# Layer 0 of a graph kernel: residual attention and the first convolution's tail written as one unrolled program over pairs of tiles

## The chip, the cores and the metric

The kernel runs on one core of a Trainium2 chip. The metric is the device time of one execution in microseconds, with the inputs already in HBM. The core has five engines that run their own instruction streams and meet at semaphores: TensorE (PE, with its weight loads PEld), VectorE (DVE), ScalarE (ACT), GpSimd (POOL) and SyncE (SP), which here only issues DMAs.

## The reference

3125 nodes with 256 features pass two layers. The change touches two blocks of layer 0, which both start from the same normalised rows `xn`:

```python
# residual attention ("mix"), linear attention with 8 heads of 32
t  = q @ kv / (q @ ksum + 1e-6)                    # q = elu(xn Wq) + 1
x1 = layer_norm(t + xn, ln1_g, ln1_b)
h  = gelu(x1 @ W1 + b1)
mix = layer_norm(h @ W2 + b2 + x1, ln2_g, ln2_b)

# two graph convolutions ("gnn"); the narrow width is 64
h  = (1 + eps_down) * (xn @ W1_down) + A @ (xn @ W1_down)
h  = relu(layer_norm(h, lng_down, lnb_down)) @ W2_down
x  = layer_norm(relu(h + xn + dir_emb[0]), ln1_g, ln1_b)   # the "down" tail ends here
h  = ... the same with A transposed, x @ W1_up, eps_up, W2_up ...
x  = layer_norm(relu(h + x + dir_emb[1]), ln2_g, ln2_b)    # the "up" tail

x_out = x_in + gnn + mix
```

The aggregation `A @ y` of the first convolution is computed while the adjacency tiles are built, before the two blocks here. After them comes the aggregation with the transposed adjacency, then the up tail, then experts, and a second layer of another make. Between the down tail and the next aggregation the new rows are multiplied by `W1_up` and the 64-wide result is split into three bf16 parts.

## The kernel before

The nodes are 25 tiles of 125 rows (`TILES`, `ROWS`), handled in 5 groups of 5 tiles (`GROUP`). The program is a row of stages. Each stage allocates its own memory and semaphores, opens with a barrier of all engines, and runs one instruction stream on each engine. The streams are loops on the chip: `overlapped` and `two_by_two` unroll two groups in a loop body, so that buffers alternate.

The stages around the change are, in order: `build_adjacency`, `mix_tail_l0` (tensors called mix_...), `gin_tail` with way "down" (gin_down_...), `gin_up` (up_...), and `gin_tail` with way "up" (gin_up_...). The mix stage starts with 8 loads of weights on SP and the down stage with 8 more. The engines of a stage wait for the last of its loads.

In `mix_tail_l0` VectorE divides the attention output by its denominators (L471 to L476), adds `XN` (L482), normalises, and later adds the MLP's output to the residual (L490), adds b2 (L493), normalises again and adds into `X` (L497). In `gin_tail` VectorE forms the hidden rows (L1050), normalises them, applies relu (L1054), and later adds the base rows (L1067), applies relu (L1071), normalises, moves the narrow product out of PSUM (L1079) and splits it (L124 to L130).

A normalisation is `layer_norm_stats` (L101, L104, L106: statistics, their aggregate, variance plus epsilon) and `layer_norm_affine`: for each tile one VectorE instruction subtracts the mean and multiplies by the gain (L113), ScalarE takes the square root of the group's variances (L507, L1094, L1103), VectorE takes the reciprocal (L115), and one more instruction for each tile multiplies by it and adds the shift (L118). GpSimd only copies slices of the queries (L451), adds the direction row (L1008) and copies rows out (L1013). The order on every engine is the order in which the code issues it; there is no scheduler.

## Time and profile before

| | us |
|---|---|
| median of 3 runs (2787.97 to 2790.32) | 2789.17 |
| the profiled execution, its own time | 2778.03 |
| its span, first to last instruction | 2776.3 |

Engine busy shares of the whole span: PE 76%, PEld 61%, DVE 58%, ACT 32%, POOL 12%. The mean granted TensorE clock is 0.848 of full speed. The profiled execution is 11 us shorter than the median of the runs, so differences are worked out inside the profile and then taken from the median. Stages follow one another at barriers, so the time of one stage adds to the total and the shares of the whole span say little about it; the stages are read one by one.

### The profile page before, as it was taken

What the parts mean: (1) busy time and instruction counts of PE and PEld (TensorE: products, weight loads), DVE (VectorE), ACT (ScalarE), POOL (GpSimd) and SP (SyncE); (2) the same over time, 40 slices, a digit from 0 to 9 for tenths busy, and PEclk for the clock granted to TensorE, in tenths of its full rate; (3) what the DMA queues carried; (4) which work ended last, traced back from release to release, by engine and by line L of the source; (5) the groups of instructions that cost most, each with busy time, mean ns of one, the idle gap of its engine ahead of it and who ended that gap; (6) DMA issues with size and microseconds to landing.
All of it is one profiled execution on the core that took longest, in us unless ns stands there. A gap on an engine that the chain in (4) does not pass through costs nothing. (4 is left out here: it accounts for less than half of the span.)

```text
span 2776.3 us, 43161 instructions
## 1 busy us (share of the span) xinstructions
PE 2098.0 (76%) x12626; PEld 1692.8 (61%) x12626; DVE 1600.5 (58%) x4311; ACT 902.2 (32%) x1696; POOL 336.9 (12%) x379
## 2 busy tenths in 40 slices
PE   7768887553577324899649779975999976899992
PEld 4446665342443214788526557754888865899992
DVE  4489997676720877322167622226999947344444
ACT  4335555121100011366425100004666631333330
POOL 0000000000100100344200000000000000333330
PEclk9889999676568555799869999988999985899996
DMA  2023333000045024122230033310222133422115
GB/s 59 10 79 113 125 122 124 17 0 9 0 124 160 6 69 118 44 66 65 59 87 0 6 104 90 90 53 25 56 57 66 34 98 130 159 93 70 48 43 150
DMA packets 90526, 196.52 MB, mean 71 GB/s; under 512 B 13526, under 2 KB 56267, under 8 KB 90452
## 3 DMA queue, kind: packets, MB, share of 16 engines
q1 hardware_dynamic: 75662, 161.01, 20.2%
q0 software_dynamic: 11520, 31.47, 3.6%
q10 hardware_dynamic: 3270, 3.20, 0.4%
q8 instruction: 28, 0.46, 0.1%
q14 instruction: 46, 0.38, 0.0%
HBM read 131.25 MB, written 64.39 MB: 70 GB/s over the span
## 5 line engine op out<-in xcount | busy, mean ns | idle before, releaser
L1572 PEld LDWEIGHTS experts_ps_h<-experts_xt,experts_up 128*128 128x128 f32 x2944 | 346.7, 194 | 28.2 <-issue 24.9
L1572 PE MATMUL experts_ps_h<-experts_xt,experts_up 128*128 128x128 f32 x2944 | 356.1, 278 | 4.4 <-ACT experts_xt L1606 2.5
L2221 PE MATMUL gat_ps_o<-Y,gat_prob_t 125*125 125x256 f32 x1250 | 273.9, 379 | 0.0
L1663 DVE COPY experts_up<-up 128x1024 f32 (+1 forms) x184 | 122.7, 696 | 243.6 <-ACT experts_hid L1616 167.1
L2221 PEld LDWEIGHTS gat_ps_o<-Y,gat_prob_t 125*125 125x125 f32 x1250 | 232.7, 188 | 33.7
L827 PE MATMUL adj_ps_w<-adj_one_k,adj_one_s 128*125 128x500 bf16 x1000 | 178.4, 305 | 80.2 <-DVE adj_one_k L758 57.8
L1584 PE MATMUL experts_ps_o<-experts_down,experts_hid 128*128 128x256 f32 x960 | 226.8, 380 | 0.3 <-ACT experts_hid L1616 0.3
L1901 PE MATMUL gcn_ps_a<-Yp,gcn_adj 125*125 125x512 bf16 x625 | 206.2, 383 | 20.9 <-DMA gcn_adj<-adjacency 11.0
L1584 PEld LDWEIGHTS experts_ps_o<-experts_down,experts_hid 128*128 128x128 f32 x960 | 173.2, 190 | 19.2 <-issue 0.5
L1631 ACT ACTIVATE experts_down<-down 128x1024 f32 (+1 forms) x120 | 138.8, 1157 | 138.9 <-DVE experts_out L1680 76.3
L827 PEld LDWEIGHTS adj_ps_w<-adj_one_k,adj_one_s 128*125 128x125 bf16 x1000 | 98.4, 138 | 130.3 <-DVE adj_one_k L758 58.0
L1902 PE MATMUL gcn_ps_b<-Yp,gcn_adj 125*125 125x256 bf16 x625 | 171.4, 274 | 0.0
L758 DVE TENSOR_SCALAR adj_one_k<-adj_key_row,adj_key_here 128x625 bf16<-128x625 f16 x500 | 159.7, 382 | 0.0
L1540 POOL DMA_INDIRECT pair<-experts_out,slot_dst x120 | 118.4, 986 | 326.4 <-DVE experts_out L1683 190.7
L1533 POOL DMA_INDIRECT experts_rows<-expert_rows,slot_src x120 | 117.2, 977 | 266.5 <-SPq L1486 127.9
L771 ACT ACTIVATE adj_tile<-adj_ps_w 125x500 bf16<-125x500 f32 x250 | 95.7, 437 | 153.9 <-PE adj_ps_w L827 153.9
L1606 ACT ACTIVATE experts_xt<-experts_ps_t 128x256 f32<-128x256 f32 x120 | 45.0, 375 | 264.9 <-PE experts_ps_t L1561 264.9
L1901 PEld LDWEIGHTS gcn_ps_a<-Yp,gcn_adj 125*125 125x125 bf16 x625 | 86.0, 138 | 73.3 <-issue 15.0
L1673 DVE TENSOR_TENSOR experts_hid<-experts_gate,experts_ps_h 128x512 f32<-128x512 f32 x64 | 44.0, 687 | 138.6 <-ACT experts_gate L1622 138.6
L2191 ACT ACTIVATE gat_prob_t<-gat_ps_t 125x500 f32<-125x500 f32 (+1 forms) x175 | 79.2, 566 | 120.1 <-PE gat_ps_t L2214 120.0
L1913 DVE TENSOR_TENSOR gcn_acc<-gcn_ps_a,Y 125x256 f32<-125x256 f32 x25 | 10.6, 424 | 166.8 <-PE gcn_ps_b L1902 166.8
L397 PE MATMUL front_ps_kv<-front_wkv,front_xt 128*125 128x512 f32 x200 | 98.1, 614 | 0.0
(363 smaller groups left out, 3811.4 us busy)
## 6 DMA issues: line engine op xcount, KB each, us to landing
adjacency<-adj_tile SPq DMA_DIRECT2D x25, 683.6 KB
adjacency_t<-adj_tile_t SPq DMA_DIRECT2D x25, 683.6 KB
up_adj_t<-adjacency_t SPq DMA_DIRECT2D x25, 683.6 KB
gcn_adj<-adjacency SPq DMA_DIRECT2D x25, 683.6 KB
cnt<-adjacency_t SPq DMA_DIRECT2D x25, 683.6 KB
up<-in_L_ffn_w SPq DMA_DIRECT2D x32, 512.0 KB, 4.7
combine_got<-pair SPq DMA_DIRECT2D x20, 560.0 KB
down<-in_L_ffn_w SPq DMA_DIRECT2D x16, 512.0 KB, 6.7
```

The lines of the kernel that those rows point to most:

```text
L397: last = nc.tensor.matmul(ps_kv[u % 2][0:ROWS, :], xt[b][:, k, cols], wkv[:, k, :], start=(k == 0), stop=(k == KC - 1))
L758: v.tensor_scalar(one_k[half][:, j, :], key_row[:], key_here[half][:, j:j + 1], None, ALU.is_equal).then_inc(one_ready, 1)
L827: last = nc.tensor.matmul(banks[bank][0:ROWS, 0:z - a], ones, keys[:, a:z], start=start, stop=stop)
L1533: nc.gpsimd.indirect_dma_start(out=rows[t % 8][:], out_offset=None, in_=table, in_offset=bass.IndirectOffsetOnAxis(ap=K.slot_src[:, t:t + ...
L1540: nc.gpsimd.indirect_dma_start(out=K.pair[:], out_offset=bass.IndirectOffsetOnAxis(ap=K.slot_dst[:, t:t + 1], axis=0), in_=out[t % 4][:], ...
L1572: last = nc.tensor.matmul(ps[:, h * 128:(h + 1) * 128], w[:, k * H + h * 128:k * H + (h + 1) * 128], xt[b][:, k, :], start=(k == 0), stop= ...
L1584: last = nc.tensor.matmul(ps_o[b][:, 0:C], hid[b][:, h * 128:(h + 1) * 128], downs[b][:, h * C:(h + 1) * C], start=(h == 0), stop=(h == HB ...
L1631: nc.scalar.activation(downs[r % 2][:], X.downs[:, bass.ds(place, 1), :].rearrange("p e w -> p (e w)"), ACT.Copy).then_inc(down_copied, 1)
L1663: last = nc.vector.tensor_copy(ups[r % 2][n][:], X.ups[n][:, bass.ds(place, 1), :].rearrange("p e w -> p (e w)"))
L1901: nc.tensor.matmul(ps_a[b][0:ROWS, :], w, K.Yp[:, s, 0:512], start=(s == 0), stop=(s == TILES - 1))
L1902: last = nc.tensor.matmul(ps_b[b][0:ROWS, 0:C], w, K.Yp[:, s, 512:768], start=(s == 0), stop=(s == TILES - 1))
L2221: last = nc.tensor.matmul(ps_o[b][0:ROWS, 0:C], prob_t[:, s * ROWS:(s + 1) * ROWS], K.Y[:, s, :], start=(s == 0), stop=(s == TILES - 1))
```

## The change

`mix_tail_l0` and the down half of `gin_tail` are gone. In their place `mix_and_down` runs both blocks in one stage, without loops on the chip. It works on pairs of tiles: 13 of them (`N`), the last a single tile. Every engine's stream is written as slots, `for s in range(-3, N + 6)`, and a slot holds the steps of different pairs (s + 3 to s - 5), so that a step's input was made some slots ago.

- The weights and vectors of both blocks (17 loads, class `MixDown`) are issued on SP at the start of `build_adjacency`, into memory of their own, and waited for at its end.
- VectorE takes the moments of each normalisation. GpSimd computes the inverse root, (variance + epsilon) to the power -0.5, in one instruction (L720 of the changed kernel). VectorE multiplies it by the negative mean. ScalarE then normalises, one activation for each tile with these two as scale and bias.
- Gain and shift of the mix normalisation, of the hidden one and of the down tail's are applied by ScalarE when it moves the transposed rows out of PSUM, where they are per-partition values. Where the rows are also needed untransposed, GpSimd multiplies by the gain (L728, L733, L744). The shifts are folded into rows added elsewhere: b2 and ln1_b enter the MLP's second matmul as a product with a row of ones, ln1_b of the convolution and ln2_b of the mix block are added to the up tail's vectors.
- GpSimd also adds into `X` (L738) and adds the direction row (L750). ScalarE moves the narrow product out of PSUM (L685, L686).
- `gin_up_tail` is the old tail's "up" half, with two more loads and two small additions at its start.

```diff
-            mix_tail_l0(nc, K, D)
-            gin_tail(nc, K, "gin_down", D, "down", K.XN, K.X1)
+            mix_and_down(nc, K, D)
             gin_up(nc, K)
-            gin_tail(nc, K, "gin_up", D, "up", K.X1, None)
+            gin_up_tail(nc, K, D)
...
+            def moments(s, n, src, which):
+                dve.drain()
+                for u in range(n):
+                    v.bn_stats(stats[:, u, :], src[:, u, :])
+                dve.drain()
+                for u in range(n):
+                    v.bn_aggr(mv[:, u, :], stats[:, u, :])
+                dve.drain()
+                v.tensor_scalar(neg[which][:, s % 4, 0:n], mv[:, 0:n, 0], -1.0, None, ALU.mult)
+                v.tensor_scalar(var[which][:, s % 4, 0:n], mv[:, 0:n, 1], LN_EPS, None,
+                                ALU.add).then_inc(var_ready[which], 1)
+
+            def shifts(s, which):
+                n = tiles(s)[1]
+                dve.wait_ge(rstd_ready[which], s + 1 + START)
+                v.tensor_tensor(shift[which][:, s % 4, 0:n], neg[which][:, s % 4, 0:n], rstd[which][:, s % 4, 0:n],
+                                ALU.mult).then_inc(shift_ready[which], 1)
...
+            for s in range(-3, N + 6):
+                if live(s + 3):
+                    hidden(s + 3)
+                if live(s - 3):
+                    shifts(s - 3, OUT)
+                if live(s - 2):
+                    moments(s - 2, tiles(s - 2)[1], res[(s - 2) % 3], OUT)
+                if live(s - 1):
+                    shifts(s - 1, ROW)
+                if live(s + 1):
+                    add_input(s + 1)
+                if live(s + 3):
+                    moments(s + 3, tiles(s + 3)[1], hid[(s + 3) % 3], HID)
+                if live(s + 1):
+                    moments(s + 1, tiles(s + 1)[1], att[(s + 1) % 3], MIXED)
+                if live(s + 2):
+                    shifts(s + 2, HID)
+                if live(s + 1):
+                    rows(s + 1)
+                if live(s - 5):
+                    split(s - 5)
+                if live(s):
+                    relu(s)
+                    moments(s, tiles(s)[1], row[s % 3], ROW)
+                if live(s + 1):
+                    shifts(s + 1, MIXED)
+                if live(s + 2):
+                    heads(s + 2)
+                if live(s - 1):
+                    residual(s - 1)
...
+            def normalise(s, dst, src, which, done):
+                act.wait_ge(shift_ready[which], s + 1 + START)
+                for u in range(tiles(s)[1]):
+                    last = nc.scalar.activation(dst[:, u, :], src[:, u, :], ACT.Identity,
+                                                bias=shift[which][:, s % 4, u:u + 1],
+                                                scale=rstd[which][:, s % 4, u:u + 1])
+                last.then_inc(done, 1)
...
+            for s in range(-3, N + 6):
+                if live(s - 4):
+                    rows_turned(s - 4)
+                if live(s + 1):
+                    hidden(s + 1)
+                if live(s - 1):
+                    mixed_turned(s - 1)
+                if live(s - 5):
+                    narrow(s - 5)
+                if live(s):
+                    mixed(s)
+                if live(s + 1):
+                    hidden_turned(s + 1)
+                if live(s - 3):
+                    out(s - 3)
+                if live(s - 1):
+                    gelu(s - 1)
+                if live(s - 1):
+                    rows(s - 1)
...
+            def root(s, which):
+                n = tiles(s)[1]
+                pool.wait_ge(var_ready[which], s + 1 + START)
+                p.tensor_tensor(rstd[which][:, s % 4, 0:n], var[which][:, s % 4, 0:n], half[:, 0:n],
+                                ALU.pow).then_inc(rstd_ready[which], 1)
...
+            for s in range(-3, N + 6):
+                if live(s - 1):
+                    root(s - 1, ROW)
+                if live(s - 4):
+                    add_out(s - 4)
+                if live(s):
+                    mixed_gain(s)
+                if live(s - 2):
+                    root(s - 2, OUT)
+                if live(s - 3):
+                    out_gain(s - 3)
+                if live(s + 3):
+                    root(s + 3, HID)
+                if live(s + 1):
+                    root(s + 1, MIXED)
+                if live(s - 1):
+                    row_gain(s - 1)
+                if live(s + 3):
+                    direction(s + 3)
...
+            for s in range(-3, N + 6):
+                if live(s - 1):
+                    up(s - 1)
+                if live(s):
+                    turn(s, ps_m, z1[s % 2], z1_done, x1t_done, m_done)
+                if live(s + 1):
+                    rows(s + 1)
+                if live(s - 3):
+                    turn(s - 3, ps_g, zr[(s - 3) % 3], zr_done, xt_done, g_done)
+                if live(s - 4):
+                    narrow(s - 4)
+                if live(s + 2):
+                    attention(s + 2)
+                if live(s - 1):
+                    out(s - 1)
+                if live(s + 2):
+                    hidden(s + 2)
```

The four loops over `s` are, in this order, those of VectorE, ScalarE, GpSimd and TensorE.

On VectorE, in `mix_tail_l0`, one group of 5 tiles is normalised like this in the kernel before (mix_x_1 is the normalised buffer):

```order
L482 TENSOR_TENSOR mix_att<-mix_att,XN 125x1280
L101 BN_STATS mix_stats<-mix_att 125x6 x5
L104 BN_AGGR mix_mv<-mix_stats 125x2 x5
L106 TENSOR_SCALAR mix_var_eps<-mix_mv 125x5
L113 SCALAR_TENSOR_TENSOR mix_x_1<-mix_att,mix_mv,mix_vec 125x256 x5
L114 REGISTER_ALU
L115 RECIPROCAL mix_rstd<-mix_std 125x5
L118 SCALAR_TENSOR_TENSOR mix_x_1<-mix_x_1,mix_rstd,mix_vec 125x256 x5
```

and a pair of the changed kernel, in the middle of a full slot, like this:

```order
L540 TENSOR_TENSOR md_att<-md_att,XN 125x512
L505 BN_STATS md_stats<-md_hid 125x6 x2
L508 BN_AGGR md_mv<-md_stats 125x2 x2
L510 TENSOR_SCALAR md_neg<-md_mv 125x2
L511 TENSOR_SCALAR md_var<-md_mv 125x2
L505 BN_STATS md_stats<-md_att 125x6 x2
L508 BN_AGGR md_mv<-md_stats 125x2 x2
L510 TENSOR_SCALAR md_neg<-md_mv 125x2
L511 TENSOR_SCALAR md_var<-md_mv 125x2
L517 TENSOR_TENSOR md_shift<-md_neg,md_rstd 125x2
L564 TENSOR_TENSOR md_row<-md_ps_w,md_base 125x512
```

The two passes over the rows (L113, L118) are gone from VectorE; a multiplication of two columns (L517) has come, and steps of other pairs stand between the moments and it.

On GpSimd the whole work of one group in the down stage is, in the kernel before (the ISA row is a wait):

```order
L1008 ISA
L1008 TENSOR_TENSOR gin_down_base_d<-XN,gin_down_direction 125x1280
L1012 REGISTER_ALU
L1013 REGISTER_ALU
L1013 COPY X<-gin_down_row 125x1280
```

and one slot of the changed kernel has this (in order: direction, root, add_out, mixed_gain, root, out_gain, two roots, row_gain; X stands for `X` in L738 and for `X1` in L744):

```order
L750 TENSOR_TENSOR md_base<-XN,md_wide 125x512
L720 TENSOR_TENSOR md_rstd<-md_var,md_half 125x2
L738 TENSOR_TENSOR X<-X,md_z_1 125x512
L728 TENSOR_TENSOR md_zg<-md_z_1,md_wide 125x512
L720 TENSOR_TENSOR md_rstd<-md_var,md_half 125x2
L733 TENSOR_TENSOR md_z_0<-md_z_0,md_wide 125x512
L720 TENSOR_TENSOR md_rstd<-md_var,md_half 125x2 x2
L744 TENSOR_TENSOR X<-md_zr,md_wide 125x512
```

GpSimd has gone from two instructions a group to five wide ones and four roots a pair, all in one queue, and the roots stand between the wide ones.

## Rows read from the trace of the kernel before

**Rows 1.** Busy time by engine in three stretches: mix stage, gap, down stage.

```profile
core 0: us, PE busy (x) PEld busy (x) DVE busy (x) ACT busy (x) POOL busy (x), PEclk, DMA share, GB/s
...
497.00:656.00 159.00, 87.19 (x330) 65.42 (x330) 118.09 (x360) 31.69 (x61) 3.68 (x3) 0.70 0.00 0
656.00:667.00 11.00, 0.00 (x0) 0.00 (x0) 0.00 (x0) 0.00 (x0) 0.00 (x0) 0.50 0.18 53
667.00:794.00 127.00, 62.53 (x225) 50.29 (x225) 91.08 (x277) 12.79 (x40) 21.49 (x10) 0.50 0.00 0
```

**Rows 2.** Timeline at the ends of the two stages (start, duration, instruction, idle before).

```profile
485.19 0.42 SPq L440 DMA_DIRECT2D mix_w<-in_L_mix_W  x1
...
497.11 2.12 PE L532 MATMUL mix_ps_a<-kv,QT 128*125 128x132 f32 x8 [19.38 <-DMA mix_vec<-in_L_mix_b]
...
793.01 0.49 DVE L130 TENSOR_TENSOR Yp<-gin_down_rest,Yp 125x320 bf16<-125x320 f32 x1
794.95 0.33 SPq L56 DMA_DIRECT2D up_adj_t<-adjacency_t  x1
```

**Rows 3.** Timeline of SP's transfers around the start of the adjacency stage.

```profile
128.76 0.42 SPq L622 DMA_DIRECT2D adj_dst_rows_i<-in_dst_rows  x1
166.66 0.36 SPq L56 DMA_DIRECT2D adjacency<-adj_tile  x1
```

**Rows 4.** Timeline of VectorE, one normalisation of the mix stage.

```profile
506.30 1.73 DVE L101 BATCH_NORM_STATS2 mix_stats<-mix_att 125x6 f32<-125x256 f32 x5
508.10 0.44 DVE L104 BATCH_NORM_AGGREGATE mix_mv<-mix_stats 125x2 f32<-125x6 f32 x5
508.62 0.17 DVE L106 TENSOR_SCALAR mix_var_eps<-mix_mv 125x5 f32<-125x5 f32 x1
508.70 2.06 DVE L113 SCALAR_TENSOR_TENSOR mix_x<-mix_att,mix_mv,mix_vec 125x256 f32<-125x256 f32 x5
```

**Rows 5.** Groups of instructions in the mix stage (busy us, mean ns).

```profile
L490 DVE TENSOR_TENSOR mix_att<-mix_ps_o,mix_x 125x256 f32<-125x256 f32 x25 | 10.6, 424 | 24.8 <-PE mix_ps_o L552 24.8
...
L507 ACT ACT_TABLE_LOAD x6 | 7.7, 1283 | 30.2 <-DVE mix_var_eps L106 30.1
L482 DVE TENSOR_TENSOR mix_att<-mix_att,XN 125x1280 f32<-125x1280 f32 x5 | 7.6, 1524 | 0.9 <-issue 0.8
```

**Rows 6.** Groups of instructions in the down stage.

```profile
L1008 POOL TENSOR_TENSOR gin_down_base_d<-XN,gin_down_direction 125x1280 f32<-125x1280 f32 x5 | 15.4, 3080 | 117.3 <-SPq L972 117.3
...
L1067 DVE TENSOR_TENSOR gin_down_row<-gin_down_ps_o,gin_down_base_d 125x512 f32<-125x512 f32 (+1 forms) x15 | 9.0, 602 | 13.8 <-PE gin_down_ps_o L1127 13.8
...
L1071 DVE TENSOR_SCALAR gin_down_row<-gin_down_row 125x1280 f32<-125x1280 f32 x5 | 4.1, 827 | 0.5
...
L126 DVE TENSOR_TENSOR gin_down_rest<-Y,Yp 125x320 f32 (+1 forms) x5 | 2.5, 492 | 0.4
```

**Rows 7.** Groups of GpSimd, whole span.

```profile
L674 POOL TENSOR_TENSOR adj_two_parts<-adj_parts 125x64 f32<-125x64 f32 x25 | 10.8, 432 | 300.4 <-ACT adj_parts L789 300.4
```

**Rows 8.** Timeline of VectorE and GpSimd together, down stage.

```profile
690.07 1.25 POOL L1013 COPY X<-gin_down_row 125x1280 f32 x1 [19.72 <-DVE gin_down_row L118]
690.14 1.52 DVE L1050 SCALAR_TENSOR_TENSOR gin_down_hid<-Y,gin_down_eps,AGG 125x320 f32 x1 [0.23 <-issue]
691.28 3.13 POOL L1008 TENSOR_TENSOR gin_down_base_d<-XN,gin_down_direction 125x1280 f32<-125x1280 f32 x1
...
693.07 1.38 DVE L106 TENSOR_SCALAR gin_down_var_eps<-gin_down_mv 125x5 f32<-125x5 f32 x1
```

**Rows 9.** Timeline of the up tail: the hidden rows with GpSimd idle.

```profile
917.19 0.55 DVE L1050 SCALAR_TENSOR_TENSOR gin_up_hid<-Y,gin_up_eps,AGG 125x320 f32 x1 [1.53 <-PE gin_up_ps_h L1119]
```

**Rows 10.** Timeline of TensorE: an MLP product at full clock, three products at half.

```profile
518.05 4.41 PE L157 MATMUL mix_ps_t<-mix_x1t,mix_w 128*128 128x500 f32 x16
...
677.12 4.62 PE L1127 MATMUL gin_down_ps_o<-gin_down_w,gin_down_hid_t 64*125 64x256 f32 x10 [0.91 <-ACT gin_down_hid_t L1097]
...
690.04 2.34 PE L139 MATMUL gin_down_ps_t<-ident_f,gin_down_row 125*128 125x125 f32 x10 [8.30 <-DVE gin_down_row L118]
...
693.87 4.46 PE L1140 MATMUL gin_down_ps_y<-gin_down_wy,gin_down_xt 128*125 128x64 f32 x20 [1.49 <-ACT gin_down_xt L148]
```

More of the change, by code:

```diff
@@ L503, in _ @@
[L503 to L518 removed]
+            p = nc.gpsimd
@@ new lines, in direction @@
+            def direction(s):
+                t, n = tiles(s)
+                if s >= 3:
+                    pool.wait_ge(row_done, s - 2 + START)
+                p.tensor_tensor(base[s % 3][:, 0:n, :], K.XN[:, t:t + n, :], wide(3, s), ALU.add).then_inc(base_done, 1)
+            for s in range(-3, N + 6):
[17 more added lines that the diff above has]
+                    direction(s + 3)
@@ new lines, in hidden @@
+            def hidden(s):
+                pe.wait_ge(zh_done, s + 1 + START)
+                if s >= 1:
+                    pe.wait_ge(hid_t_done, s + START)
+                if s >= 6:
+                    pe.wait_ge(y_done, s - 5 + START)
+                for u in range(tiles(s)[1]):
+                    last = nc.tensor.transpose(ps_s[0:64, u * ROWS:(u + 1) * ROWS], zh[s % 2][:, u, :],
+                                               K.ident_f[0:ROWS, 0:ROWS])
+                last.then_inc(hid_done, 1)
@@ L965, in _, with gin_up_tail @@
                                         AX.X, ALU.add)
-def gin_tail(nc, K, stage, D, way, base, out):
-    first = way == "down"
+def gin_up_tail(nc, K, D):
     with ExitStack() as st:
-        m = Memory(nc, st, stage)
+        m = Memory(nc, st, "gin_up")
         w2 = m.sb("w2", (64, C))
-        wy = m.sb("wy", (128, KC, 64))
         eps1 = m.sb("eps1", (ROWS, 1))
@@ L1042, in _ @@
             v.tensor_scalar(eps1[:], eps1[:], 1.0, None, ALU.add)
-            if first:
-                v.memset(K.Yp[:, :, 192:256], 0.0)
+            v.tensor_tensor(direction[:], direction[:], extra[:, 0, :], ALU.add).then_inc(joined, 1)
+            v.tensor_tensor(wide[:, 1, :], wide[:, 1, :], extra[:, 1, :], ALU.add)
             dve.drain()
```

470 lines of the change are left out of this document (290 added, 180 removed).

## The prediction, on record before the changed kernel ran

> **What bounds the kernel now.** I read the busy times by stretch first, since stages meet at barriers. The mix stage computes from 497 to 656 us and the down stage from 667 to 794, with 11 us of nothing but loads between them and 12 ahead of the first [rows 1, 2]. In both VectorE is the busiest engine: 118.1 of 159 us and 91.1 of 127, against TensorE's 87.2 and 62.5 [rows 1]. The views of waits and the timelines say what the rest is: VectorE waits 24.8 us for the MLP's last product and 13.8 us for the down stage's rows [rows 5, 6], because within a group of five tiles the steps follow one another and little of the next group is mixed in. The region that the change replaces, from the first load at 485.19 to the first transfer of the next stage at 794.95 [rows 2], lasts 309.8 us.
>
> **What VectorE does after the change.** A full slot handles one pair of tiles in each step. Its price, from rows, with 0.07 us for each gap behind a drain (506.30 + 1.73 to 508.10) [rows 4]:
>
> - Moments of 256 columns: five statistics take 1.73 us, so two about 0.74 (the first costs a bit more than the following ones); aggregates of two 0.23 (of five 0.44); negative mean and variance 0.25 together (one is 0.17); three gaps 0.22 [rows 4]. That is 1.44, three times 4.32. With 64 columns I take 1.04. Together 5.36.
> - Four multiplications of two columns, like L106's 0.17 with a little for their waits: 0.8 [rows 4].
> - Hidden rows of 128 columns: 320 columns take 0.55 with GpSimd idle [rows 9], so 0.34.
> - Adding the input, 512 columns: 1280 take 1.52, about 1.04 ns for a column and 0.18 fixed [rows 5]: 0.71, with its gap 0.78.
> - Residual and base rows out of PSUM, 512 columns each: 15 instructions took 9.0 us, ten of them with 512 columns and five with 256, so 0.69 and 0.42 [rows 6]: 1.38.
> - Relu of 512 columns: 1280 take 0.83 [rows 6], so 0.43 and 0.07: 0.50.
> - Splitting: three operations of 128 columns, L126 with 320 took 0.49 [rows 6], so 0.29 each and two gaps: 1.07.
> - Heads: an operation of 256 columns out of PSUM takes 0.42 (L490) [rows 5], two overlapped 0.8; denominators, reciprocal and gaps 0.5: 1.31.
>
> The sum is 11.54 us a pair. For 12.5 pairs that is 145 us where VectorE is busy 209.2 now [rows 1]. The difference is mainly L113 and L118, 2.06 us for five tiles each [rows 4], three times over the wide rows and once over the narrow. To 11.54 I add 0.5 for some 15 satisfied waits.
>
> **What GpSimd's new work costs VectorE.** A wide operation of GpSimd takes 3.08 us for 1280 columns and 0.43 for 64 [rows 6, 7], so 1.3 for 512; five make 6.5 us a slot. The power has no row. Its floor is the 0.2 us that the smallest operations take; upward I take 0.43, the small addition [rows 7], for the sum, and say below where it would hurt. So GpSimd needs 8.2 us of a slot and isn't the bound. But it blocks VectorE. At 690.14 the hidden rows took 1.52 us instead of 0.55 while a GpSimd copy ran to 691.32, and at 693.07 L106 took 1.38 instead of 0.17, until GpSimd's addition ended at 694.41 [rows 4, 8, 9]; the statistics between them were not slowed. So an operation of VectorE of either kind waits for the whole GpSimd instruction. Going through a slot in program order I find four such meetings. mixed_gain becomes free when residual ends and takes its turn just ahead of the first shifts: 1.25. out_gain ends during the hidden moments: 0.5. row_gain and direction stand back to back where the split wants to run: 0.8 and 1.2. add_out falls under heads, which read PSUM, and costs nothing. That is 3.75, less 0.2 each (the rows show a little less delay than overlap), so 3.0 us a slot. Bounds: 0, and 6.5 if all five block fully. I take 3.0 since each meeting follows from the order.
>
> The Trainium skill (SBUF — State Buffer, Who interferes with whom) says the same in general, that VectorE instructions with two SBUF inputs or in a two-port mode and GpSimd's exclude each other for a whole instruction; by it the additions of two SBUF tensors block as well, which no row here shows clearly, and the sum would keep its 3.0. Against the change stands its page GPSIMD Engine Reference, Engine selection: two-input elementwise work is about twice as slow on GpSimd and belongs on VectorE. The rows agree on the price, 3.08 us against 1.52 for 1280 columns [rows 5, 6]. What they make of it here: kept on VectorE, the five would cost 5 x 0.71 = 3.6 us a slot, against 3.0 of blocking, so moving them gains little; the gain comes from L113 and L118, which go to ScalarE.
>
> **A slot, and the stage.** 11.5 + 0.5 + 3.0 = 15.0 us. Twelve full pairs 180, the single last tile 8.4, the operations ahead of the loop 1.3. The first slots have enough steps of their own to keep VectorE busy. In the last ones only chains are left (transposes, move, narrow product, move, split): some 6 us idle. Stage: 196 us.
>
> **The cover.** ScalarE has 17 activations a slot, about 7 us, and its table of functions is changed once, where the square root's alone was loaded six times (1.28 us each [rows 5]). TensorE's products a slot have 3576 columns, 8 + 2 transposes and 4 narrow products. At half clock (each product is recorded twice) 1280 columns took 4.62 us, ten transposes 2.34, ten narrow products 4.46 [rows 10]: 12.9 + 2.3 + 1.8 = 17.0. At full clock 2500 columns took 4.41 [rows 10], so about 8.4. The granted clock was 0.70 in the mix stage with PE busy 55% and 0.50 in the down stage with 49% [rows 1], so I expect about 0.75 and some 11 us a slot, hidden. The chain through the engines is covered too: out(s - 1) can start some 3 us into VectorE's slot, when gelu is done, and is wanted at 14.3; even at half clock it takes 5.5. The roots of MIXED are wanted 4 us after their variance.
>
> **The ends.** Loads: they move to `build_adjacency`, where SP issues nothing between 129.2 and 166.7 us [rows 3], so they cost nothing there; 485.19 to 497.11, 11.9 us, goes [rows 2], less 1.6 for opening the stage with 23 more semaphores (an estimate: 0.07 us each, from the two stages before and after the down stage, which open 2.1 and 1.5 us after the last operation with 18 and 9 semaphores). The gap between the stages, 11 us [rows 1], goes entirely. 1.5 us from the last operation to the next stage stay [rows 2]. After: 1.6 + 196 + 1.5 = 199, so the region falls by 111. The up tail gets two more loads, two additions of 0.42 and a change of table: +2. Net -109. The profiled execution would be 2778 - 109 = 2669, the median **2680**.
>
> **Rivals.**
> - GpSimd doesn't get in the way: 0 instead of 3.0 a slot, 39 us less, 2641. For it: half of VectorE's slot reads PSUM or takes statistics. Against: rows 8.
> - TensorE sets the pace, at half clock throughout: 17.0 and one wait of 1.4, so about 18 a slot, +3 in twelve slots: 2717. For it: the down stage never got above 0.50 [rows 1]. Against: such a TensorE would never pause, and it was granted 0.70 and more when it was busy 55%.
> - The roots are late, a wait in place of the removed one: power, signal and queue on GpSimd put some 3 us on two of the four chains of a slot, 20 to 21 us a slot: about 2750. For it: a root stands behind wide operations.
> - Slower than before: the power is a long routine on GpSimd. VectorE's slot would have to reach 15.0 + 109/12.5 = 23.7 us; GpSimd reaches that when four powers take 23.7 - 6.5 = 17.2 us, 4.3 us each, ten times the small addition. With 6 us each a slot is 30.5, so 15.5 x 12.5 = 194 more than forecast: 2874. Against: it handles two columns.
> - The stage is as long as before, since work only moved: would need 24 us a slot with nothing in the rows to fill it.
>
> **How the numbers follow.** VectorE bound with blocking, slots of 13.5 to 17.5 us, 2660 to 2712: 0.65. No blocking, 2641: 0.10. TensorE at 2717: 0.10. Late roots, 2750: 0.09. Slower: 0.05. Unchanged: 0.01. The range takes the first three and the bounds of their terms: 2640 to 2728, and leaves out the last three. 0.2% (5.6 us) is about what a measurement of this kernel can tell from no change. Faster 0.94, within it 0.01, slower 0.05.
>
> **What the new profile would show.** A stage of about 196 us between the adjacency's end and the next aggregation; VectorE without long waits in it, some 165 to 190 us busy because blocked instructions read longer; the first shifts and the split at over 1 us where GpSimd's gain runs; bn_stats at 0.41 unchanged; powers near 0.4; TensorE's clock near 0.75; no load wait in front. The prediction is wrong if VectorE's waits for ScalarE or GpSimd (L517) come to more than 1 us a slot, if a power takes over 2 us, or if SP's added loads delay the adjacency's first steps.

## The result and the profile after

The changed kernel takes **2664.44 us** (median of 4 runs, 2661.84 to 2667.41) against 2789.45 for the kernel before on the same chip: a ratio of 0.9553 with a 95% interval of 0.9538 to 0.9567. The prediction was 2680 with a range of 2640 to 2728, so the sign and most of the mechanism were right, and the forecast time was 15.6 us too long.

The kernel before was profiled a second time (e9 below), and this execution, 2790.22 us, is nearer to the median than the first. The comparison below uses it. These are busy times by stretch, cut at the same places in both kernels: the replaced stages (from their first load, or the merged stage's first VectorE operation), the next aggregation, the up tail's loads, the up tail, and the rest. The columns are the stretch, its length, the busy time of each engine with its instructions, the granted TensorE clock, the DMA share and GB/s. First the kernel before, second execution:

```profile
486.10:795.67 309.57, 149.63 (x555) 115.83 (x555) 209.32 (x637) 44.47 (x101) 26.40 (x14) 0.60 0.02 6
795.67:903.61 107.94, 95.75 (x403) 44.97 (x403) 3.88 (x7) 3.15 (x7) 0.00 (x0) 0.85 0.70 181
903.61:913.63 10.02, 0.00 (x0) 0.00 (x0) 0.16 (x2) 0.00 (x0) 0.00 (x0) 0.50 0.16 51
913.63:1010.67 97.04, 30.85 (x75) 18.30 (x75) 83.88 (x255) 5.78 (x20) 15.23 (x5) 0.50 0.00 0
1010.67:2788.50 1777.83, 1451.65 (x8659) 1245.72 (x8659) 929.27 (x2185) 611.84 (x1041) 254.15 (x263) 0.88 0.26 73
```

The changed kernel:

```profile
488.26:662.97 174.71, 147.84 (x629) 106.81 (x629) 151.77 (x514) 93.49 (x218) 115.02 (x118) 0.79 0.00 1
664.54:772.26 107.72, 93.86 (x403) 44.74 (x403) 3.88 (x7) 3.15 (x7) 0.00 (x0) 0.86 0.70 182
772.26:785.02 12.76, 0.00 (x0) 0.00 (x0) 0.82 (x3) 1.28 (x1) 0.04 (x1) 0.50 0.18 60
785.02:881.52 96.50, 30.85 (x75) 18.37 (x75) 83.56 (x255) 5.79 (x20) 15.13 (x5) 0.50 0.00 0
881.52:2660.10 1778.58, 1452.08 (x8659) 1246.68 (x8659) 929.30 (x2185) 612.14 (x1041) 255.03 (x263) 0.88 0.25 73
```

The next aggregation starts at 664.54 instead of 795.67, 131.1 us earlier. The 309.6 us became 174.7, and 1.6 more to the next stage's first transfer; of what that saves, 2.0 are lost because the stage takes longer to open and 0.2 because the adjacency ends later. The aggregation itself is the same, 107.9 and 107.7. The up tail's loads take 12.8 instead of 10.0, its work half a microsecond less, and what follows to the end of the execution's own time 0.8 more (1780.3 against 1779.5). 131.1 + 0.2 + 0.5 - 2.7 - 0.8 = 128.3; the two executions differ by 2790.22 - 2661.84 = 128.4. VectorE's busy time in the stage fell from 209.3 to 151.8 us and TensorE's did not change (149.6 and 147.8). TensorE is now busy 85% of the stage instead of 48%, and its granted clock went from 0.60 to 0.79. VectorE is busy 87%.

Of the 134.9 us between 309.6 and 174.7, 57.5 are VectorE's busy time and 77.4 its idle time: the loads at the two places ([rows 1, 2]: 11 us and 12) and, for the larger part, waits for other engines within a group of tiles. No run here prices the pairs and slots apart from the rest; e5 below, with the normalisation back on VectorE, is still 94.8 us shorter than the old stages.

The loads cost the adjacency little, but not nothing. VectorE's first cast behind the adjacency's own three loads, first in e9 and then in the changed kernel:

```profile
132.55 0.38 DVE L685 CAST adj_src_f<-adj_src_i 128x420 f32<-128x420 int32 x1 [7.53 <-DMA adj_dst_rows_i<-in_dst_rows]
...
132.96 0.38 DVE L999 CAST adj_src_f<-adj_src_i 128x420 f32<-128x420 int32 x1 [8.31 <-DMA adj_dst_rows_i<-in_dst_rows]
```

The first of those loads is issued at 128.13 in e9 and at 127.84 in the changed kernel, so the cast comes 4.4 us behind it before and 5.1 us after: the 17 loads queued behind them delay the adjacency's first steps by 0.7 us. Its last operation on GpSimd starts at 480.30 in e9 and at 480.45 here, which is 0.4 us later counted from the first load. That operation, and VectorE's first of the merged stage:

```profile
480.45 0.19 POOL L992 COPY DEG<-adj_parts 125x1 f32<-125x1 f32 x1
...
488.26 0.15 DVE L498 TENSOR_SCALAR md_eps<-md_eps 125x1 f32<-125x1 f32 x1 [14.85 <-PEq L85]
```

One VectorE slot, from one residual addition to the next (start, duration):

```profile
584.82 0.68 DVE L548 TENSOR_TENSOR md_res<-md_ps_o,md_zg 125x512 f32<-125x512 f32 x1
585.42 0.34 DVE L555 SCALAR_TENSOR_TENSOR md_hid<-Y,md_eps,AGG 125x128 f32<-125x128 f32 x1
585.68 1.24 DVE L517 TENSOR_TENSOR md_shift<-md_neg,md_rstd 125x2 f32<-125x2 f32 x1
587.02 0.75 DVE L505 BATCH_NORM_STATS2 md_stats<-md_res 125x6 f32<-125x256 f32 x2
...
588.56 0.69 DVE L540 TENSOR_TENSOR md_att<-md_att,XN 125x512 f32<-125x512 f32 x1
...
590.08 0.37 DVE L510 TENSOR_SCALAR md_neg<-md_mv 125x2 f32<-125x2 f32 x1
...
592.93 1.14 DVE L577 CAST Yp<-md_rest 125x128 bf16<-125x128 f32 x1
594.15 1.22 DVE L579 TENSOR_TENSOR Yp<-md_rest,Yp 125x128 bf16<-125x128 f32 x1
...
598.55 0.68 DVE L548 TENSOR_TENSOR md_res<-md_ps_o,md_zg 125x512 f32<-125x512 f32 x1
```

GpSimd in the same slot:

```profile
584.35 1.27 POOL L738 TENSOR_TENSOR X<-X,md_z 125x512 f32<-125x512 f32 x1
585.64 1.27 POOL L728 TENSOR_TENSOR md_zg<-md_z,md_wide 125x512 f32<-125x512 f32 x1
588.49 0.70 POOL L720 TENSOR_TENSOR md_rstd<-md_var,md_half 125x2 f32<-125x2 f32 x1 [1.57 <-DVE md_var L511]
589.15 1.27 POOL L733 TENSOR_TENSOR md_z<-md_z,md_wide 125x512 f32<-125x512 f32 x1
...
592.73 1.27 POOL L744 TENSOR_TENSOR X<-md_zr,md_wide 125x512 f32<-125x512 f32 x1
593.95 1.27 POOL L750 TENSOR_TENSOR md_base<-XN,md_wide 125x512 f32<-125x512 f32 x1
```

The slot lasts 13.73 us and VectorE has no wait in it. Four VectorE instructions are long: a shift of two columns takes 1.24 us beside `mixed_gain`, L510 0.37 at the end of `out_gain`, the two last operations of the split 1.14 and 1.22 beside `row_gain` and `direction`. [rows 8] showed the same in the kernel before, once with each kind of instruction. Beside a power (588.49) an addition of 512 columns took its usual 0.69. VectorE's only waits for another engine behind its first instruction of the stage all fall in the drain, the last slots in which few steps are left (engine, line, what for: us in total, times, longest):

```profile
DVE md_res L548 <- PE md_ps_o L814: 2.6, 3, 1.1
```

GpSimd's powers, from the groups of instructions of the stage (busy us, mean ns | idle before):

```profile
L720 POOL TENSOR_TENSOR md_rstd<-md_var,md_half 125x2 f32<-125x2 f32 (+1 forms) x52 | 35.9, 690 | 53.1 <-DVE md_var L511 53.1
```

### The profile page after: what moved, and what is told of

Same layout as the page of the kernel before. It is cut to its first block and busy times, and to the rows that moved or that the text cites. A ratio compares the mean times of both kernels' runs of the same rounds, so it can differ in the third digit from the quotient of the medians.

```text
span 2660.1 us, 43432 instructions
## 1 busy us (share of the span) xinstructions
PE 2101.0 (79%) x12700; PEld 1688.1 (63%) x12700; DVE 1544.3 (58%) x4190; ACT 952.5 (36%) x1814; POOL 426.6 (16%) x483
## 5 line engine op out<-in xcount | busy, mean ns | idle before, releaser
L1943 DVE TENSOR_TENSOR experts_hid<-experts_gate,experts_ps_h 128x512 f32<-128x512 f32 x64 | 44.0, 687 | 140.1 <-ACT experts_gate L1892 129.8
L2183 DVE TENSOR_TENSOR gcn_acc<-gcn_ps_a,Y 125x256 f32<-125x256 f32 x25 | 10.6, 424 | 166.0 <-PE gcn_ps_b L2172 166.0
```

## Experiments

All but e9 are edits of the changed kernel. The median is of four runs; the ratio is to runs of the kernel before on the same chip, which had medians of 2788.6 to 2791.7. "Stage" is from VectorE's first operation to its last (174.7 us in the changed kernel), in one profiled execution of each kernel. How well it repeats can be seen from e4, whose stage is the same program from its first VectorE operation on: 174.8. A full slot is one in which every step has a pair; it is read from one residual addition to the next. In this table clock and busy times are of the stage. e3 and e12 leave work out and do not compute the reference's result.

| | median us | ratio, 95% | stage us | full slot us | PE / DVE busy us | clock |
|---|---|---|---|---|---|---|
| changed kernel | 2664.4 | 0.9538 to 0.9567 | 174.7 | 13.7 to 14.0 | 147.8 / 151.8 | 0.79 |
| e1 shifts later | 2661.6 | 0.9524 to 0.9565 | 177.2 | 13.1 to 14.0 | 146.8 / 145.7 | 0.80 |
| e2 split first | 2665.0 | 0.9530 to 0.9573 | 177.4 | 11.6 to 14.3 | 146.6 / 140.1 | 0.81 |
| e3 short GpSimd | 2634.7 | 0.9426 to 0.9462 | 146.9 | 10.6 to 10.9 | 127.8 / 121.4 | 0.91 |
| e4 loads back | 2674.0 | 0.9567 to 0.9602 | 174.8 | 13.7 to 14.0 | 148.0 / 151.9 | 0.79 |
| e5 normalise on VectorE | 2701.2 | 0.9663 to 0.9712 | 214.8 | 16.9 to 17.3 | 154.1 / 190.5 | 0.75 |
| e6 roots twice | 2671.4 | 0.9567 to 0.9618 | 182.6 | 14.1 to 14.4 | 149.3 / 157.6 | 0.78 |
| e7 = e2, up twice | 2660.3 | 0.9527 to 0.9582 | 171.7 | 12.6 | 148.2 / 142.3 | 0.93 |
| e8 all on VectorE | 2667.7 | 0.9550 to 0.9597 | 183.4 | 13.8 to 14.1 | 149.8 / 157.9 | 0.79 |
| e10 up twice alone | 2662.7 | 0.9518 to 0.9566 | 174.1 | 13.7 to 14.1 | 150.8 / 152.6 | 0.90 |
| e11 direction on TensorE | 2686.5 | 0.9596 to 0.9654 | 193.7 | 11.9 to 15.3 | 175.5 / 135.4 | 0.75 |
| e12 no bias product | 2659.7 | 0.9518 to 0.9550 | 171.5 | 12.6 | 131.9 / 142.3 | 0.78 |

### e3: how much GpSimd's wide operations cost VectorE

```diff
-                p.tensor_tensor(zg[s % 2][:, 0:n, :], z1[s % 2][:, 0:n, :], wide(0, s), ALU.mult)
+                p.tensor_tensor(zg[s % 2][:, 0:n, 0:2], z1[s % 2][:, 0:n, 0:2], wide(0, s), ALU.mult)
 (the same in the other four; base, zg and X1 are filled with zeros at the stage's start)
```

> Leaves work out: GpSimd's five wide operations handle 2 columns of a tile instead of 256; the rest of their outputs is filled with zeros once at the stage's start (3 to 6 us, which the trace shows apart). Theory A (3.1 us a slot of blocking): VectorE's slot falls to about 10.6 us, the stage by 39 us before the filling, 2630. Rival (forecast: no blocking): 2664 plus the filling, 2668. Theory C (TensorE close behind): slots of 11.6 us with VectorE waiting for TensorE, 2640.

The same place in the slot, VectorE, with short GpSimd operations:

```profile
576.27 0.23 DVE L579 CAST Yp<-md_rest 125x128 bf16<-125x128 f32 x1
576.57 0.29 DVE L581 TENSOR_TENSOR Yp<-md_rest,Yp 125x128 bf16<-125x128 f32 x1
...
580.04 0.68 DVE L550 TENSOR_TENSOR md_res<-md_ps_o,md_zg 125x512 f32<-125x512 f32 x1
...
580.90 0.17 DVE L519 TENSOR_TENSOR md_shift<-md_neg,md_rstd 125x2 f32<-125x2 f32 x1
...
590.93 0.68 DVE L550 TENSOR_TENSOR md_res<-md_ps_o,md_zg 125x512 f32<-125x512 f32 x1
```

The shift takes 0.17, the cast 0.23, the subtraction 0.29, and the slot 590.93 - 580.04 = 10.89. It is the fourth full slot; the third, which answers to the one shown above, takes 10.60 instead of 13.73. On average the four full slots take 10.7 instead of 13.8, 3.1 us less. With the filling the first hidden rows come 4.1 us after the stage's first operation instead of 1.8, so without it the stage would last 146.9 - 2.3 = 144.6 us. GpSimd's wide operations cost the stage 174.7 - 144.6 = 30.1 us. VectorE's busy time fell by as much (30.4) and its waits for TensorE hardly changed (2.6 and 3.1). The rival without blocking is out. So is another, that the roots behind the wide operations come late: the views of waits show VectorE waiting for no root in the changed kernel.

### e1 and e2: moving VectorE's work out of the meetings

e1 puts the moments of OUT, which begin with statistics, under `mixed_gain`. e2 also puts the split ahead of `rows` and the heads behind it, so that `row_gain` and `direction` run under operations that read PSUM (the second block gives the order in words):

```diff
-                if live(s - 3):
-                    shifts(s - 3, OUT)
                 if live(s - 2):
                     moments(s - 2, tiles(s - 2)[1], res[(s - 2) % 3], OUT)
+                if live(s - 3):
+                    shifts(s - 3, OUT)
...
-order: rows, split, relu and moments ROW, shifts MIXED, heads, residual        (changed kernel, e1)
+order: split, rows, heads, relu and moments ROW, shifts MIXED, residual        (e2)
```

> In VectorE's slot the first shifts (OUT) change places with the moments of OUT, nothing else. Theory A (GpSimd's wide instruction blocks VectorE's instructions with two SBUF inputs, the statistics are free): the 1.24 us of that L517 falls to 0.15, since mixed_gain now runs under bn_stats and bn_aggr; the slot goes from 13.75 to about 12.7 us and the kernel from 2664 to about 2651. Theory B (that L517 is long because the root comes late, not because of the port): the slot stays at 13.75, 2664. Theory C (TensorE, busy 147.8 us of the stage's 174.7, is close behind): VectorE's wait for the MLP's product (L548) takes the place of most of it, 2660.

> The edit of e1, and the split goes ahead of rows, the heads ahead of relu, so that row_gain and direction run under rows and heads, which read PSUM. Theory A: L577 and L579, 1.15 and 1.21 us now, fall to about 0.2 and 0.3, relu may be held up for 0.4: 1.5 us a slot beside e1's 1.1, slots of about 11.2 us, 2632. Theory B (no port): no change, 2664. Theory C (TensorE close behind, 147.8 us busy at a granted clock of 0.79): slots no shorter than 11.6 to 12 us, with waits of VectorE for TensorE, 2640 to 2645, or a higher granted clock, and then as A.

The edits did to VectorE what was expected: 6 and 12 us less busy. In e2:

```profile
573.90 1.15 DVE L510 TENSOR_SCALAR md_neg<-md_mv 125x2 f32<-125x2 f32 x1
...
579.62 0.23 DVE L577 CAST Yp<-md_rest 125x128 bf16<-125x128 f32 x1
...
582.15 0.71 DVE L570 TENSOR_SCALAR md_row<-md_row 125x512 f32<-125x512 f32 x1
...
586.08 0.69 DVE L548 TENSOR_TENSOR md_res<-md_ps_o,md_zg 125x512 f32<-125x512 f32 x1 [1.69 <-PE md_ps_o L814]
```

The split is short again. But L510, a multiplication with one input, became 1.15 us under `mixed_gain`, and L570 0.71 under `direction`: part of the blocking only moved. (In e1 L510 of the hidden moments takes 0.87 us under `out_gain` instead of 0.37, so half of what the shift gave came back.) And VectorE waits for the MLP's product, 1.69 us at 586.08. The waits by what was waited for:

```profile
DVE md_res L548 <- PE md_ps_o L814: 11.8, 5, 3.3
...
DVE md_den L527 <- PE md_ps_a L780: 3.2, 4, 1.4
```

So the 12 us went to TensorE (15.0 us of waits instead of 2.6), and the kernels are as fast as the changed one (e1 2661.6, e2 2665.0, within what can be told apart). Most of these waits stand at the ends of the stage: 5.2 us up to the first residual addition and 7.6 at the last three, against 1.7 in the full slots. The full slots did become shorter, 12.8 us on average instead of 13.8, and the ends longer. In the 10 us before 586.08 and in the 10 before the first residual addition (523.89, waited for 2.6 us) TensorE was busy without a pause at a granted clock of 0.50. Theory A is right about the blocking of the moved instructions. Theory C is right that TensorE takes what is freed; e1 came out at the 2660 that it said, e2 20 us above its 2640 to 2645, since it had not seen what the ends would lose.

### e7, e10, e12: what TensorE is short of

e7 (on e2) and e10 (on the changed kernel) compute the MLP's first product twice; e12 (on e2) leaves out the product that adds the bias row.

```diff
 e7, e10
-                for h in range(KC):
+                for h in range(2 * KC):
+                    h = h % KC
 e12
-                    nc.tensor.matmul(bank, K.ones[0:1, 0:ROWS], crow[:], start=True, stop=False)
```

> e2_split_first with the MLP's first product computed twice into the same banks: more work for TensorE and nothing else (about 1.1 us more at full clock a slot, 2.3 at half). Theory C1 (in e2 TensorE ended last because its clock fell whenever it ran out of work; busier, it is granted 1.00): granted clock 0.9 or more through the stage, VectorE's 12 us of waits for L814 fall to 5, and the kernel is faster than e2's 2665: 2650. Theory C2 (TensorE is simply the bound there): slots longer by 1 to 2 us, 2680. Theory D (something else equalises the stage): 2665.

> The changed kernel in its own order, with the MLP's first product computed twice: more TensorE work alone. Theory C (there VectorE is the bound until the drain, TensorE is hidden at whatever clock): granted clock 0.9, slots still 13.7, the drain shorter or longer by 2 us, 2664 within 4. Rival (TensorE holds the stage already): 2.3 us a slot more at half clock, up to 2690, or less if the clock rises: 2655.

> e2_split_first without the product of one partition that adds the bias row to the MLP's output (L812, 25 tiles, 19.9 us busy over e2's stage); the row is left out of the result. Theory (in e2's order TensorE ends last in places, so what e1 and e2 freed on VectorE was lost to it): VectorE's 12 us of waits for L814 and 3 for L780 fall by half or more, stage 177 to about 168, kernel 2655. Rival 1 (with less to do TensorE is granted less, and the wait stays): clock under 0.80, 2665. Rival 2 (TensorE at the pace throughout): stage 20 us shorter, 2645.

Busy times of the stage, in the columns of before. e2:

```profile
488.41:665.77 177.36, 146.56 (x629) 105.89 (x629) 140.12 (x514) 92.82 (x218) 115.21 (x118) 0.81 0.00 1
```

e7:

```profile
489.39:661.09 171.70, 148.15 (x733) 110.90 (x733) 142.30 (x514) 92.70 (x218) 115.22 (x118) 0.93 0.00 1
```

e12:

```profile
488.21:659.74 171.53, 131.91 (x579) 104.08 (x579) 142.34 (x514) 92.70 (x218) 115.17 (x118) 0.78 0.00 1
```

In e7 TensorE runs 52 more products (each is recorded twice, x733 against x629) and is busy only 1.6 us longer than in e2, because it is granted 0.93 instead of 0.81. The slots become an even 12.6 us and VectorE's waits for L814's product fall from 11.8 to 5.6 us. Doing more made the stage 5.7 us shorter. Leaving work out (e12: 14.7 us less busy, clock 0.78) makes it 5.8 us shorter as well. Both say that in e2 TensorE ended last in places, and the rows above that it did so at half clock. By clock and waits e7 is theory C1, though the kernel takes 2660.3 where 2650 was expected; e12 halves the waits as its theory said (7.0 us instead of 15.0), while the clock fell to 0.78 as its rival 1 had it, and the stage is 171.5 us where 168 was expected. In the changed kernel's own order the same doubling lifts the clock from 0.79 to 0.90 and changes nothing (174.7 and 174.1 us, 2664.4 and 2662.7): there VectorE sets the pace. In whole times e7 can't be told from e2: the medians differ by 0.2%, taken on two chips, and the ratios to the kernel before are the same (0.9555 and 0.9551). The stage, the waits and the clock, each from one profiled execution, carry the finding.

e7's full slots are 1.1 to 1.4 us shorter than the changed kernel's, which is 5 us over four of them. The last three slots, where few steps are left and VectorE waits 3.1 and 2.6 us for the MLP's product, take 23.5 us instead of 19.7. That is why a slot 1.2 us shorter is worth only 3 us of stage.

### e11: the direction row through TensorE

```diff
+                    nc.tensor.matmul(ps_w[0:ROWS, u * C:(u + 1) * C], K.ones[0:1, 0:ROWS], W.flat[:, 2, :],
+                                     start=True, stop=False)
-                                base[s % 3][:, 0:n, :], ALU.add)
+                                K.XN[:, t:t + n, :], ALU.add)
```

> The order of e2, and the direction row is added in TensorE's products of the rows (one more product of one partition and 256 columns a tile) instead of by GpSimd, so rows add XN itself; the loads stay 17. Theory (blocking by one GpSimd operation of 1.27 us a slot goes, and TensorE, with 0.5 to 1.2 us more work a slot, keeps its clock): granted clock 0.9, VectorE's slot 11.6 to 12.0 instead of 12.6, stage 160 to 167 us instead of 177, 2650. Rival 1 (TensorE at half clock ends last, and now has more to do): 2668 to 2675. Rival 2 (the blocking moves to the next operation): stage 171, 2660.

The stage of e11 by busy times:

```profile
488.68:682.42 193.74, 175.47 (x679) 120.26 (x679) 135.37 (x514) 93.28 (x218) 99.63 (x105) 0.75 0.00 1
```

Its two products of the rows, from the groups of instructions:

```profile
L834 PE MATMUL md_ps_w<-md_wg,md_hid_t 64*125 64x256 f32 x50 | 20.5, 495 | 0.0
L832 PE MATMUL md_ps_w<-md_flat,ones 1*125 1x256 f32 x50 | 20.4, 493 | 0.6 <-ACT md_hid_t L667 0.6
```

VectorE's waits in it for TensorE:

```profile
DVE md_res L549 <- PE md_ps_o L812: 21.5, 7, 5.8
...
DVE md_row L564 <- PE md_ps_w L834: 7.4, 4, 2.8
...
DVE md_den L528 <- PE md_ps_a L778: 6.7, 7, 1.4
```

Rival 1 by its mechanism: TensorE ends last and has more to do. The time, 2686.5, lies beyond its 2668 to 2675. A product with a single row of weights costs as much as one with 64 (L832 493 ns, L834 495 a record), 20.4 us in all for 25. The granted clock was 0.75, against 0.81 in e2, and VectorE waits 35.6 us for TensorE. In e7 added products had raised the clock to 0.93. Whether it is their kind (one row against 128) or their place that makes the difference wasn't tried and stays open.

### e8: the five wide operations on VectorE

```diff
-    (GpSimd) mixed_gain(s), out_gain(s - 3), add_out(s - 4), row_gain(s - 1), direction(s + 3)
+    (VectorE) direction(s + 3), out_gain and add_out(s - 4), row_gain(s - 2) first in the slot,
+              mixed_gain(s) ahead of heads
```

> The five wide operations go from GpSimd to VectorE, GpSimd keeps the roots alone. Prediction's step (moving them gains little): 5 x 0.70 = 3.5 us more VectorE work a slot against 2.9 us of blocking that goes (slot 13.75 against 10.89 with short GpSimd operations): slot 14.4, 8 us more over the stage, 2672. Rival (GpSimd's help is worth its whole VectorE price): 3.5 x 12.5 = 44 us more, 2708. Rival 2 (the blocking costs more than is read, by what it does to TensorE's clock): equal or faster, 2655 to 2664.

No VectorE instruction is blocked any more, and each of the five takes 0.66 to 0.67 us on average over twelve pairs and the single tile (L594 is one, L517 the shifts; groups of the stage):

```profile
L594 DVE TENSOR_TENSOR X<-X,md_z 125x512 f32<-125x512 f32 (+1 forms) x13 | 8.7, 673 | 1.3 <-issue 0.4
...
L517 DVE TENSOR_TENSOR md_shift<-md_neg,md_rstd 125x2 f32<-125x2 f32 (+1 forms) x52 | 8.0, 154 | 0.3 <-issue 0.2
```

The stage is 183.4 us, 8.7 more than with GpSimd, where 8 was expected. The whole kernel's median is 3 us higher, and the intervals of the two ratios overlap, so by whole times the two can't be told apart. What GpSimd does for VectorE here, 43.1 us of VectorE's time (five times 8.6 or 8.7), it takes back in good part by 30.1 us of blocking. The balance of these two would be 13.0 us, and the stage shows 8.7; where the other 4.3 are was not traced. The prediction weighed the Trainium skill (GPSIMD Engine Reference, Engine selection), which puts two-input elementwise work on VectorE. On the price the rows agree: 512 columns take 1.27 us on GpSimd and 0.69 on VectorE (L540). On the choice this run does not, since here VectorE is the bound, but only by 8.7 us of the stage.

### e5 and e6: ScalarE's and GpSimd's parts

e5 normalises on VectorE, right after the shift; e6 takes each root twice.

```diff
 e5
+                for u in range(n):
+                    last = v.tensor_scalar(dst[:, u, :], src[:, u, :], rstd[which][:, s % 4, u:u + 1],
+                                           shift[which][:, s % 4, u:u + 1], ALU.mult, ALU.add)
 e6
+                p.tensor_tensor(scratch[:, which, s, 0:n], var[which][:, s % 4, 0:n], half[:, 0:n], ALU.pow)
```

> The three wide normalisations (MIXED, OUT, ROW) go from ScalarE back to VectorE, but as one operation a tile with both scalars (multiply by the root, add the shift), right behind the shift; the gains stay on GpSimd and in the columns. Theory 1 (the gain came from splitting gain and bias off, not from ScalarE as such): 256 columns cost about 0.24 us (L570 takes 0.43 for 512), six of them and three gaps 1.7 us a slot, 21 us over the stage, 2685. Theory 2 (the prediction's: what goes to ScalarE is worth what L113 and L118 cost, 0.41 us an operation and more where GpSimd blocks them): 3 to 5 us a slot, 2700 to 2725. Rival 3 (TensorE is what ends last): no more than 5 us, 2669.

> Every root is taken twice on GpSimd, first into a buffer that nobody reads, so each comes 0.69 us later and GpSimd has 2.8 us more a full slot (9.1 to 11.8 of 13.75). Theory (roots hidden, GpSimd not a bound): 2664 within 5; the power is no port user, since L540 ran beside one in 0.69. Rival (roots are nearly late, four chains a slot): VectorE waits at L517, up to 2.8 us a slot, 2664 + 34 = 2698. Rival 2 (the wide operations slide under other VectorE work): a few us either way.

VectorE in e5, a pair of normalisations and the addition behind it:

```profile
587.14 0.74 DVE L538 TENSOR_SCALAR md_zr<-md_row,md_rstd,md_shift 125x256 f32<-125x256 f32 x2
587.97 1.59 DVE L562 TENSOR_TENSOR md_att<-md_att,XN 125x512 f32<-125x512 f32 x1
```

VectorE in e6, the hidden rows and the relu:

```profile
574.93 1.00 DVE L556 SCALAR_TENSOR_TENSOR md_hid<-Y,md_eps,AGG 125x128 f32<-125x128 f32 x1
...
584.72 1.34 DVE L571 TENSOR_SCALAR md_row<-md_row 125x512 f32<-125x512 f32 x1
```

In e5 two operations take 0.74 us, not the 0.48 that theory 1 took from L570 (one alone takes 0.41 us for 256 columns with two per-partition scalars, where the relu takes 0.43 for 512). Three pairs with their gaps are 2.5 us a slot, and new meetings such as L562 at 587.97 (1.59 instead of 0.69) bring it to 3.2. The stage grows by 40.1 us, the kernel by 36.8. At 2701.2 it lies in theory 2's 2700 to 2725 and 16 us above theory 1's 2685: taking the three wide normalisations off VectorE is worth 40 us of stage, and one combined operation instead of two would have bought only a part of what went. e6's 2671.4 lies outside the 2664 within 5 that was expected; it is its rival 2. The later roots are waited for 1.5 us in all. The stage still grows by 7.8 us, since GpSimd's wide operations slide to other neighbours (L556 1.00 instead of 0.34, L571 1.34 instead of 0.43). The power itself is hidden; the place of what stands behind it isn't.

### e4 and e9: the loads, and the aggregation

```diff
 e4
-            K.md.load(sp, weights_in)          (in build_adjacency)
+            W.load(sp, w_in)                   (at the start of mix_and_down, VectorE waits for it)
```

> The 17 loads of the merged stage are issued at its own start instead of among the adjacency's first ones. Theory (the loads were 12 us of waiting and cost next to nothing where they are now): first VectorE instruction 10 to 13 us later after the stage's opening, adjacency 1 us earlier, 2674 to 2677. Rival (they cost the adjacency as much there as they would here, or the scheduling of the DMA queues hides them): 2664 within 3.

> The kernel before once more, for a second profile. In all nine profiles of the changed kernels the aggregation behind the merged stage lasts 105 to 112 us from its first transfer to the next stage's first load, in the one profile of before 102.2. Theory (the change makes that stage start later in TensorE's clock or share memory differently): again 102 to 103. Rival (its length varies from run to run by that much): 105 or more, and the 5.5 us are not the change's.

VectorE's first operation of the stage in e4:

```profile
501.85 0.15 DVE L505 TENSOR_SCALAR md_eps<-md_eps 125x1 f32<-125x1 f32 x1 [28.76 <-DMA md_flat<-in_L_mix_shift_rows]
```

e4: VectorE starts at 501.85 instead of 488.26, and the kernel takes 2674.0, 9.6 us more. The adjacency ends 0.3 us earlier (480.31). The loads were worth 13.6 us by the start of the stage and 9.6 by the medians, and where they are now they cost some tenths of a microsecond. The theory holds. e9: the aggregation of the kernel before lasts 107.9 us this time, after 102.2 in the first profile; in the changed kernels it lasts from 105.3 to 111.9. The rival holds: the aggregation's length varies between executions, and a difference of 5 us there is no effect of the change.

## Why the prediction was right, and where it was off

- **VectorE bounds, work moves off it.** Right. But where the prediction says that the gain comes from L113 and L118, this holds for VectorE's busy time alone; the larger part of what went is its idle time (77.4 of 134.9 us), which the sum took in without a name by pricing a slot as VectorE's work only. The price of a pair was 12.04 us with the waits, 10.6 to 10.9 by e3: 14 to 18 us too much over 12.5 pairs. That error is spread over small items: waits that were satisfied cost nothing (0.5 forecast), additions out of PSUM take 0.60 from start to start instead of 0.69, the two-column multiplications 0.07 where they follow another operation, since in these rows an instruction starts before the one ahead has ended unless a drain stands between (584.82 + 0.68 against 585.42). The split's three operations and two gaps sum to 1.01 and not to the 1.07 that stands there. VectorE was busy 151.8 us, under the 165 to 190 that the new profile was to show.
- **Blocking by GpSimd.** The mechanism and the four meetings were right, at the named places: first shifts 1.09 (forecast 1.05 net), L510 0.20 (0.3), split 0.9 and 0.9 (0.6 and 1.0). The four instructions together are 3.1 us longer and a full slot 3.1 on average, forecast 3.0. The price of a wide operation, 1.3 us against 1.27 measured, was a choice and not the line through its two rows, which gives 1.4. Over the stage it is 30.1 us and not 37.5, because only five slots hold all nine steps; in the others fewer of the meetings take place. The Trainium skill (SBUF — State Buffer, Who interferes with whom) says that VectorE instructions with two SBUF inputs and the two-port forms of copies and scalar operations share ports with GpSimd's, and that whichever of the two starts first shuts the other out for its whole length. For GpSimd's wide operations the runs agree with both kinds: L517 and L579, and with one input L577, L510 and, in e2 and e6, the relu. Statistics and PSUM readers kept their times. For the power they don't agree: nine additions of 512 columns (L540, from 524.60 to 626.42) started 0.07 us into a power of 0.70, and each took 0.69.
- **Stage.** 174.7 against 196. Without blocking it is 144.6 (e3) against 158.5, so 13.9 are from the work and 7.4 from the blocking.
- **The ends.** The opening cost 2.0 (forecast 1.6). The loads cost the adjacency 0.4 us (forecast nothing), and its first steps came 0.7 us late, so one of the forecast's signs of being wrong did appear, if a small one. The rest was close: 1.5 us to the next stage were 1.57, the up tail +2.2 (forecast +2).
- **Start of the sum.** The sum was made against a profile of before that lay 11.4 us under the median. By e9 that lay in places without change, which vary from run to run: the aggregation (102.2 against 107.9) and what follows the up tail (1774.0 against 1779.5). The profile after has both at full length, 107.7 and 1780.3. So its own time is only 7 us under the forecast 2669, although the stage is 21 us shorter than forecast, and that closeness is luck; the medians differ by 125.0 where 109 had been said.
- **TensorE.** Hidden, as forecast, with a clock of 0.79 against 0.75 and 11.8 us a pair against 11. What the prediction did not see is how near it stood: it is busy 85% of the stage, and both reorderings that relieved VectorE ran into it. The rival "TensorE sets the pace" was wrong for this kernel; in e2 TensorE ended last at the ends of the stage, in e11 in some full slots too.
- **The power.** 0.69 us each, forecast 0.43. GpSimd was busy 115 us of 174.7 and no shift waited for a root, so neither late roots nor the slower case (4.3 us a power) came about.
- **Moving the gains and additions to GpSimd gains little.** Right: 8.7 us of stage by e8, where 3.6 - 3.0 = 0.6 a slot (7.5 us) had been said. That the two numbers are so close is in part luck, since e8 and e3 together leave 4.3 us open.

No version here that computes the whole result beats the changed kernel by more than can be told apart; e7 is 0.16% under its median and e1 0.11%, and their intervals hold its ratio.

## What to carry to other kernels

Price a pipelined stage by its busiest engine's instructions, start to start, and add what a second engine on the same ports blocks, meeting by meeting, in program order. Blocking counts only in the slots in which both partners are live, and moving a victim away puts another in its place unless the new one reads PSUM or takes statistics. When the bound engine is relieved, look at once at the next one, and at the first and last slots as well as the full ones: TensorE, 85% busy at a granted clock of 0.8, took everything that the reorderings freed, most of it at the two ends of the stage.

## What was not expected of the hardware

- More TensorE work can go with a shorter stage: 52 more products cost 1.6 us of busy time in e7, and the granted clock went from 0.81 to 0.93; in e10 they cost 2.9 us of busy time and none of the stage. The 25 further products of e11, of one row, went with a clock of 0.75.
- GpSimd's power of two columns takes 0.69 us, three times its smallest wide-form operation (0.20 for four columns in e3), and did not block a VectorE addition beside it (0.69 at 588.56, and eight more like it).
- VectorE's operation with two per-partition scalars takes 0.41 us for 256 columns, that with constants 0.43 for 512.
